# A graph network on one core: messages are added at the rank of their node instead of at an edge that claimed it

## The reference

```python
h = jnp.maximum(_layernorm(x), 0)
x = x + L0(src, dst, h)         # out = (msg + scaled) * dinv; msg: sum over edges, by src, of scaled[dst]
h = jnp.maximum(_layernorm(x), 0)
x = x + L1(h, [src, dst], edge_attr_4, edge_attr_16)
```

```python
r = silu(silu(silu(edge_rbf @ M1) @ M2) @ M3);  tpw = (r @ M4).reshape(-1, 4, C)
msg0 = segment_sum(m0e, rcv, n); msg1 = segment_sum(m1e, rcv, n)   # rcv is dst
A0, A1 = msg0 @ W_lin0, msg1 @ W_lin1
B0, B1 = polynomials of A0 and vv = sum(A1 * A1)
o0, o1 = B0 @ WB0 + h0 @ Wsc0, B1 @ WB1 + h1 @ Wsc1
# then mean and variance of o over all nodes, and a norm with them
```

## Time and profile before

| | us |
|---|---|
| median of 3 runs | 2388.08 (2364.14 to 2389.84) |
| the profiled execution | 2398.8, its span 2396.7 |
| PE, DVE, ACT, POOL busy | 1849.3, 1786.8, 1525.1, 1182.2 |
| DMA moved | 437.47 MB, 183 GB/s |
| granted clock of TensorE, mean | 0.904 of full |

### The profile page before, as it was taken

One profiled execution on the slowest core, in us unless ns is written; L12 is line 12 of the kernel. 1 busy time (PEld: TensorE's weight loads), 2 busy tenths in 40 slices (PEclk: granted clock), 3 DMA queues, 4 the chain that ended last, 5 costly groups with the idle time before them and its releaser, 6 DMA issues.

```text
span 2396.7 us, 54201 instructions
## 1 busy us (share of the span) xinstructions
PE 1849.3 (77%) x14326; PEld 1465.7 (61%) x14326; DVE 1786.8 (75%) x7877; ACT 1525.1 (64%) x3485; POOL 1182.2 (49%) x1159
## 2 busy tenths in 40 slices
PE   6967888888888978999996677776999677777200
PEld 4645666666665655777775566665888677777200
DVE  6764776767676756788784888885998799999663
ACT  4753655556565644777785666655999789999100
POOL 2134555545454432777774777765442121212565
PEclk9987998999899987999997999997999899999655
DMA  5673544445555433777773666655777588888775
GB/s 169 238 182 113 178 173 163 173 166 177 174 175 175 172 131 125 156 163 161 158 152 66 119 120 119 119 102 171 242 245 237 204 288 289 288 289 278 251 228 172
DMA packets 209488, 437.47 MB, mean 183 GB/s; under 512 B 51948, under 2 KB 90377, under 8 KB 209418
## 3 DMA queue, kind: packets, MB, share of 16 engines
q1 hardware_dynamic: 136730, 361.16, 44.0%
q0 software_dynamic: 59584, 74.91, 16.9%
q10 hardware_dynamic: 13104, 0.61, 0.6%
HBM read 220.08 MB, written 219.00 MB: 183 GB/s over the span
## 4 chain that ended last, share of the span: by engine, by line
PE 31%; issue 22%; ACT 18%; POOL 9%; DVE 8%; DMA 6%; another core or an unknown queue 2%; SPq 2%; ACTq 1%; DVEq 0%; POOLq 0%
PE bank L792 16%; ACT hb L1063 6%; PE bank L772 5%; POOL big L502 4%; POOL x_tab L513 3%; PE bank L788 3%; PE bank L751 2%; ACT ht L1212 2%; ACT h L1063 2%; POOL msg_tab L513 2%; PE bank L718 2%; PE bank L729 1%; DVE st L1319 1%; PE bank L736 1%
## 5 line engine op out<-in xcount | busy, mean ns | idle before, releaser
L792 PE MATMUL bank<-w_sb,ht 128*128 128x256 f32 x1568 | 448.4, 429 | 35.7 <-issue 34.5
L792 PEld LDWEIGHTS bank<-w_sb,ht 128*128 128x128 f32 x1568 | 311.3, 209 | 143.0 <-issue 104.4
L1319 DVE BATCH_NORM_STATS2 st<-big 128x6 f32<-128x256 f32 x882 | 314.5, 412 | 93.3 <-DMA big<-x_tab,idx 75.5
L1035 ACT COPY ht<-bank 128x512 f32<-128x512 f32 x196 | 107.9, 588 | 321.9 <-PE bank L772 250.3
L772 PE MATMUL bank<-ident,hb 128*128 128x128 f32 x1568 | 216.4, 281 | 96.7 <-ACT hb L1063 75.0
L1397 DVE SCALAR_TENSOR_TENSOR x1b<-bank,dinv,big 128x64 f32<-128x64 f32 x392 | 109.9, 280 | 223.2 <-PE bank L792 133.5
L502 POOL DMA_INDIRECT big<-x_tab,idx x196 | 192.8, 983 | 141.9 <-ACT h L1063 66.4
L772 PEld LDWEIGHTS bank<-ident,hb 128*128 128x128 f32 x1568 | 181.0, 144 | 131.0 <-issue 96.5
L481 POOL DMA_INDIRECT node_edge<-node_tab,idx x196 | 188.2, 960 | 132.0 <-DVE x1b L1399 74.2
L557 POOL TENSOR_TENSOR big<-big,bias 128x256 f32<-128x256 f32 x98 | 71.6, 730 | 323.5 <-ACT hb L1063 284.2
L1024 ACT ACTIVATE hb<-big,rs 128x256 f32<-128x256 f32 x392 | 207.5, 590 | 18.3 <-DVE rs L1342 16.6
(11 more groups left out here) (241 smaller groups left out, 4514.5 us busy)
## 6 DMA issues: line engine op xcount, KB each, us to landing
big<-in_x_dram SPq DMA_DIRECT2D x97, 512.0 KB
x_tab<-x1b SPq DMA_DIRECT2D x97, 512.0 KB
big<-x_tab SPq DMA_DIRECT2D x97, 512.0 KB
out_dram<-x1b SPq DMA_DIRECT2D x97, 512.0 KB, 2.9
x_odd<-x1b SPq DMA_DIRECT2D x48, 512.0 KB
big<-x_odd SPq DMA_DIRECT2D x48, 512.0 KB
msg_tab<-zeros SPq DMA_DIRECT2D x50, 256.0 KB, 2.2
tpw_tab<-tpb SPq DMA_DIRECT2D x49, 256.0 KB, 2.0
```

Of the source, the lines that this page charges most:

```text
L792: last = mm(y, ht[:, q, (2 * j + k) * P:(2 * j + k + 1) * P], w_sb[:, k, :], start=False, stop=(j == 1 and k == 1))
L1319: last = v.bn_stats(st[:, k, j, :], row)
```

## The change

- `claim_tab`, the claims, the winners, `lead`, `lead_now` and `final_idx` are gone.
- Behind the count, DVE marks the nodes that any edge ends at (`has_dst`, from bank 0). PE counts them by column (four products with one output column each, `in_column`), counts for each node the marked ones on lower partitions of its column (one product with `later`, 392 columns), and adds the marked ones of all columns before (four more products of 392 columns, with the new mask `columns_later`). The sum is the node's rank. DVE turns it into a row number that puts rank r on partition r mod 128 and edge column r // 128, and stores it as a third value in `of_node`.
- `node_tab` rows have three values. POOL gathers the 98 columns of dst rows first, copies the ranks to integers, then for each column scatters dst to `list_tab[rank]`, waiting for the last one to land, and gathers the src row: 98 scatters and 196 gathers, three a group. `list_tab` is cleared with the number of a row of `x1_tab` that holds zeros (N + 256); SP reads it back as column 0 of `idx3`.
- E2 adds messages at the rank. E3 gathers the nodes of the list, each once: the first 78 columns are full, the 79th has 83 nodes, and columns 80 to 98 all read the one row of zeros. F scatters by the list; the numbers beyond the output fall to the bounds check.

```diff
@@ named tables and tiles
-        claim_tab = dram("claim_tab", [G * NG, 1], I32)
-        node_tab = dram("node_tab", [G * NG, 2])
+        list_tab = dram("list_tab", [EDGES, 1], I32)
+        node_tab = dram("node_tab", [G * NG, 3])
+        columns_later = sb("columns_later", [G, J, G * J])
...
@@ POOL, constants before the first mark
+            const(g.memset(columns_later[:], 1.0))
...
+            const(g.affine_select(out=columns_later[:], in_=columns_later[:], compare_op=ALU.is_gt, fill=0.0, base=0,
+                                  pattern=[[-G, J], [1, G * J]], channel_multiplier=-1))
...
@@ POOL, during P1
-                if n % 4 == 0 and n // 4 > 3:
-                    pool.wait_ge(p1["x1"].sem, 2 * (n // 4 - 3))
+                if n % 3 == 0 and n // 3 > 3:
+                    pool.wait_ge(p1["x1"].sem, 2 * (n // 3 - 3))
...
+            run_written_out(T, 0, dst_step)
+            pool.wait_ge(node_in[0].sem, 16 * T)
+            settle(pool)
+            place(g.tensor_copy(rank_i[:], node_edge[:, :, 0, 2]))
+            pool.wait_ge(pre["list_cleared"].sem, 16)
...
+                pace(T + 2 * t)
+                landed(pool, list_out, s, 1)
+                pool.indirect_dma_start(list_tab, rows_of(rank_i[:, t:t + 1]), idx3[:, 1, t:t + 1], None
+                                        ).then_inc(list_out[0].sem, 16)
+                pace(T + 2 * t + 1)
+                of_node_step(1, t)
...
@@ POOL, E3 and F
-                    gather(e3_got, s, 1, x1_tab, e3_free)
+                    gather(e3_got, s, 0, x1_tab, e3_free)
-                    pool.indirect_dma_start(out, rows_of(final_idx[:, t:t + 1]), f_rows[s.slot(0, 4)][:, i, :],
+                    pool.indirect_dma_start(out, rows_of(idx3[:, 0, t:t + 1]), f_rows[s.slot(0, 4)][:, i, :],
...
@@ SP, behind the loads of the weights, and in E1
-            sp.dma_start(claim_tab.rearrange("(p a) d -> p (a d)", p=P),
-                         node_ok[:].bitcast(I32)).then_inc(pre["claim_cleared"].sem, 16)
+            sp.dma_start(list_tab.rearrange("(p a) d -> p (a d)", p=P), no_node[:]).then_inc(pre["list_cleared"].sem, 16)
+            sp.dma_start(x1_tab[N + 2 * P:N + 3 * P, :], zeros[:, 0:D]).then_inc(pre["cleared"].sem, 16)
...
+            all_landed(sp, list_out, T)
+            sp.dma_start(idx3[:, 0, :], list_tab.rearrange("(p t) d -> p (t d)", p=P)).then_inc(pre["list_in"].sem, 16)
@@ PE, between the count and P1
+            pe.wait_ge(pre["has_dst"].sem, 1)
+            for k in range(J):
+                last = mm(bank[6][0:G, k:k + 1], has_dst[:, k * G:(k + 1) * G], ones[:, 0:1], start=True, stop=True)
+            last.then_inc(pre["in_column"].sem, 1)
+            mm(bank[5][:, 0:G * J], later[:, 0, 0:P], has_dst[:], start=True, stop=False)
+            pe.wait_ge(pre["in_column_sb"].sem, 1)
+            for k in range(J):
+                last = mm(bank[5][:, 0:G * J], in_column[:, k:k + 1].to_broadcast([G, P]), columns_later[:, k, :],
+                          start=False, stop=(k == J - 1))
+            last.then_inc(pre["rank"].sem, 1)
@@ PE, E3
-                            last = mm(bank[7][to:to + 1, at], lead_now[:, s.slot(6, 4), i:i + 1],
+                            last = mm(bank[7][to:to + 1, at], ones[:, 0:1],
@@ DVE, degrees
+            v.tensor_scalar(has_dst[:], ends, 0.0, None, ALU.is_gt).then_inc(pre["has_dst"].sem, 1)
...
+            dve.wait_ge(pre["in_column"].sem, 1)
+            v.tensor_copy(in_column[:], bank[6][0:G, 0:J]).then_inc(pre["in_column_sb"].sem, 1)
             dve.wait_ge(pre["root"].sem, 1)
             link(v.reciprocal(dinv, deg[:]))
+            dve.wait_ge(pre["rank"].sem, 1)
+            v.tensor_scalar(of_node[:, :, 2], bank[5][:, 0:G * J], float(T), None, ALU.mult)
+            link(v.tensor_copy(rank_hi[:], bank[5][:, 0:G * J]))
+            link(v.tensor_scalar(rank_hi[:], rank_hi[:], 7, None, ALU.logical_shift_right))
+            link(v.scalar_tensor_tensor(out=of_node[:, :, 2], in0=rank_hi[:], scalar=float(1 - EDGES),
+                                        in1=of_node[:, :, 2], op0=ALU.mult, op1=ALU.add))
             v.tensor_tensor(dinv2[:], dinv, dinv, ALU.mult).then_inc(pre["dinv"].sem, 1)
@@ DVE, start of E1, and E3
-            dve.wait_ge(win_in[0].sem, 16 * T)
-            one(v.tensor_copy(winner[:], winner_i[:]))
-            from_trash(win_delta, winner, 1)
...
+            one(v.tensor_copy(rank[:], node_edge[:, :, 0, 2]))
+            from_trash(rank_delta, rank, 1)
-                    v.tensor_copy(lead_now[:, s.slot(3, 4), :], pair(lead, s, 3)).then_inc(e3["lead_now"].sem, 1)
```

More of the change, by code:

```diff
@@ L189, in build @@
         trash = sb("trash", [P, 2, 2])
[L190 to L193, removed]
+        no_node = sb("no_node", [P, T], I32)
+        rank_i = sb("rank_i", [P, T], I32)
+        rank = sb("rank", [P, T])
+        rank_hi = sb("rank_hi", [P, G * J], I32)
+        has_dst = sb("has_dst", [P, G * J])
+        columns_later = sb("columns_later", [G, J, G * J])
+        in_column = sb("in_column", [G, J])
         valid = sb("valid", [P, T])
@@ L229, in build @@
         deg = sb("deg", [P, G * J])
[L230 removed]
+        of_node = sb("of_node", [P, G * J, 3])
         dinv2 = sb("dinv2", [P, G * J])
@@ L352, in build @@
         EDGES_LOADED = 16 * len(edge_loads)
-        CLEARED = 16 * (S + 2)
-        pre = named("pre", "dve_chain consts edges mlp inputs prepared b3 claim_cleared cleared deg root dinv dinv_out")
+        CLEARED = 16 * (S + 3)
+        pre = named("pre", "dve_chain consts edges mlp inputs prepared b3 list_cleared cleared deg root dinv dinv_out has_dst "
+                           "in_column in_column_sb rank place list_in")
         cnt = named("cnt", "rbf onehot counted turned0 act0 layer1 act1 layer2 act2 layer3 act3 layer4 weights")
@@ L462, in pace @@
             def pace(n):
-                if n % 4 == 0 and n // 4 > 3:
-                    pool.wait_ge(p1["x1"].sem, 2 * (n // 4 - 3))
-            def claim_step(s):
-                t = s.k
-                if t == 0:
-                    pool.wait_ge(pre["prepared"].sem, 1)
-                    pool.wait_ge(pre["claim_cleared"].sem, 16)
-                    pool.wait_ge(p1["x1"].sem, 2)
-                pace(3 * t)
-                landed(pool, claim_out, s, 1)
-                pool.indirect_dma_start(claim_tab, rows_of(idx3[:, 0, t:t + 1]), edge_i[:, t:t + 1],
-                                        None).then_inc(claim_out[0].sem, 16)
-                if t == 0:
-                    pool.wait_ge(pre["dinv_out"].sem, 16)
-                for i in range(2):
-                    pace(3 * t + 1 + i)
-                    pool.indirect_dma_start(node_edge[:, t, i, :], None, node_tab, rows_of(idx3[:, i + 1, t:t + 1])
-                                            ).then_inc(node_in[0].sem, 16)
@@ new lines, in of_node_step, with dst_step @@
+            def of_node_step(i, t):
+                pool.indirect_dma_start(node_edge[:, t, i, :], None, node_tab, rows_of(idx3[:, i + 1, t:t + 1])
+                                        ).then_inc(node_in[0].sem, 16)
+            def dst_step(s):
+                pace(s.k)
+                of_node_step(0, s.k)
+            pool.wait_ge(pre["prepared"].sem, 1)
+            pool.wait_ge(p1["x1"].sem, 2)
+            pool.wait_ge(pre["dinv_out"].sem, 16)
+            run_written_out(T, 0, dst_step)
@@ L496, in gather @@
+            run_written_out(T, 0, list_step)
             def gather(got_sems, s, which, table, free):
@@ L1467, in _ @@
             dve.wait_ge(node_in[0].sem, 16 * 2 * T)
[L1468 to L1477 removed]
+            one = Chain(dve, e2["chain_d"])
+            one(v.tensor_copy(rank[:], node_edge[:, :, 0, 2]))
+            from_trash(rank_delta, rank, 1)
             def e1_step(s):
```

46 lines of the change are left out of this document (11 added, 35 removed).

## The result

The first timing gave 2253.01 us (2247.06 to 2260.07, six runs) beside 2384.05 us for before (six runs): a ratio of 0.9464, 95% interval 0.9432 to 0.9495. The forecast was 2399 us and "the same". It was wrong by 146 us, and the time fell outside its range.

What follows compares the result with a forecast made beforehand. It saw one chain until 141.6 us, then PE busiest in P1 and E3, POOL in E1, E2 and mostly F. Terms 6.7 + 6.7 - 1.2 - 1 = +11.2 us on the median 2388.08 gave 2399 us, range 2370 to 2430.

Steps and rivals of the forecast that it cites:

- P1: In P1, POOL issues 294 small DMAs instead of 392, which nobody there waits for or is slowed by: 0 us.
- Rival A: POOL's small DMAs slow P1 and a quarter fewer give back 33 us of PE's idle time: 2366 us, chance 0.12.
- The counter-argument from DVE's equal durations: DVE's 192-column operation took 0.46 us without POOL DMAs and 463 ns in P1's mean, so contention seemed unlikely.
- Constants: Before P1, two more POOL operations on 1568 columns delay SP's loads and the first store of `tpb`: +6.7 us.
- The rank: Before P1, PE's added products and DVE's operations for the rank delay the first moments: +6.7 us (+4 to +9.4).
- Into E1: Between P1 and E1, a cast and two subtraction halves remain of DVE's eight operations: -1.2 us.
- E1, E2: POOL keeps the same four DMAs a step in both stages, and rank spreads rows as src does: 0 us.
- E3: In E3, DVE loses a copy a step, but PE sets the pace: -1 us (0 to -4).
- F: In F, POOL's issue is unchanged and the last 19 scatters write nothing: 0 us (-8 to +20).
- B: In E3's last 19 columns all reads hit one zero row; at worst 85 us slower, 2484 us, chance 0.07.
- C: F is held by its writes: 2427 us, chance 0.13; sign: DVE waiting for output landings in F's first 39 steps.
- D: The preparation before P1 overlaps more than forecast: +6 us in all, 2394 us, inside the forecast, no separate chance.

Runs made afterwards that it cites:

- a_none: The kernel after with all 294 small GpSimd DMAs held until P1's last group; 2632.92 us in one run, P1 587.9 us.
- b_half: The kernel before with its four small DMAs a group released two by each half group of P1; 2359.47 us, 0.9893 of before.
- a_x16: The kernel after with a fourth small gather, of 16 rows, in each group of P1; 2418.66 us, 1.0028 of before.

## Why the prediction was wrong, and where it was right

- **P1, taken as 0: this step failed.** It rested on two stretches of the earlier trace rows, the one with 12 DMAs and PE busy for 17.0 us, the other with 8 and 12.9. "POOL follows the groups; the poor stretch had fewer DMAs" was true and proved nothing: a starved group is long, so DMAs per microsecond are few in it. What the runs showed in its place: P1 took 625.1 us for 783.9, 159 less. The number that should have been read is DMAs a group, and the order in time: behind the runs of eight DMAs in before PE's first gap comes 5.1 to 5.3 us after their start. The gaps of PE ended by "issue", 43 us in the 460 us from 240 to 700, had a row in the view of waits and none in the prediction.
- **Rival A (0.12) was the mechanism, mis-sized.** It took the price as proportional to the number of DMAs, a quarter of 131 us, 33. The runs show no price up to three a group (48.5 us for eight with none and with three) and all of it above (about 60 with four), so that a quarter fewer gave back most of it (P1 625.1 us, the floor 587.9). It gave more than the 131 us of idle time, because the products themselves got shorter: L792's busy time fell from 448.4 to 398.6 us as the clock stayed high. The counter-argument from DVE's equal durations was weak by itself, since the operation that it looked at reads one tensor from SBUF and one from PSUM, and the rule that it cites is about two SBUF inputs; a_none bears it out. But it doesn't exclude gaps between instructions, which leave durations alone.
- **Constants, +6.7: too high.** The zero product came 3.8 us later (4.6 on chip C), and so did the first store of `tpb` (35.27 for 31.47). The memset took the 1.4 expected; the affine select of 1568 columns took 1.53 us, not 4 times 1.24. Timeline of POOL, SP, ACT and PE in after, beside the earlier trace rows:

```profile
2.66 1.40 POOL L424 MEMSET columns_later<- 98x1568 f32 x1
...
6.03 1.53 POOL L432 TENSOR_SCALAR_AFFINE_SELECT columns_later<-columns_later 98x1568 f32<-98x1568 f32 x1
...
35.27 1.10 SPq L601 DMA_DIRECT2D tpw_tab<-tpb  x1
...
39.81 0.65 ACT L1007 COPY tpb<-bank 128x256 f32<-128x256 f32 x2 [5.65 <-DMA tpw_tab<-tpb]
...
140.31 1.19 PE L751 MATMUL bank<-zeros 128*128 128x256 f32 x2 [0.83 <-ACT tpb L1007]
141.29 1.38 PE L755 MATMUL bank<-ones,has_dst 128*98 128x1 f32 x8
142.53 1.66 PE L757 MATMUL bank<-has_dst,later 128*128 128x392 f32 x2
143.98 4.09 PE L760 MATMUL bank<-columns_later,in_column 98*128 98x392 f32 x8
...
151.14 1.41 DVE L1372 BATCH_NORM_STATS2 st<-big 128x6 f32<-128x256 f32 x4
```

- **The rank, +6.7: right within a microsecond.** First moments came 5.8 us later behind the zero product (5.7 on chip C). The four small products took 1.4 for 1.2, the five of 392 columns 5.5 for 6.5 (142.53 to 148.07), at a granted clock of 0.78 in the stretch.
- **Into E1, E1, E2, E3, F.** On chip C: -0.2 for -1.2; E1 +1.0 and E2 +3.3 for 0 (E2 between +1.0 and +3.3 in the six kernels profiled there, after among them); E3 with what follows +0.2 for -1; F's scatters -0.5 for 0. With 10.4 at the start and 0.7 from there to P1's end that is, but for 0.3 at the very end, the 14.6 us by which the profiled executions differ (2199.5 and 2184.9), 9.8 by the medians.
- **Rivals B and C didn't come.** E3 is as long as before. POOL waits more for the stores of the gathered rows (31.1 us for 15.9 in the 210 us of E3), and nothing comes of it. DVE does wait for landings of the output in F, the sign named for C, but before does so too (on chip C 32.9 and 32.7 us), and F's first twenty pairs of scatters stand 2.9 us apart in both. D was near on the start (+8 for 9.6 measured) and would have given 2394.

So every term but P1 was right to 4 us. That the whole fits so well on chip C, +11.2 for +9.8, is in part luck: the start was forecast 3 us too long and E2 3 us too short. On the other chips one wrong zero outweighed them all.

## What to carry to other kernels

Gaps that end in "issue" on several engines at once are a cost with a cause elsewhere: look at what another engine issued in the microseconds before, and count it per unit of work, not per microsecond. If a kernel runs indirect DMAs of GpSimd under dense work of TensorE, spread them to the units of that work, and time it on more than one chip: here a change is worth 5.5% or nothing by the chip. When such DMAs are held back, find out what then comes last; twice here the gain went into the tail ahead of the next stage.

## What the runs showed of the hardware

- On chips A and B and in the first pair, four indirect DMAs of GpSimd in a group of 6 us starve TensorE, down to one matmul in 0.7 us, and VectorE shows "issue" gaps beside it (29 us in the 460 from 240 to 700 in before, 9 in after). With three, or on chip D with three and one plain DMA, they don't. 16 rows and 128 rows count alike. On chip C nothing of it shows at 320 DMAs in 460 us.
- The price begins just above three a group: 48.5 us for eight groups with 24 DMAs, 48.5 to 53.6 with 25 to 28, about 60 with 32. It costs the granted clock too (1.00 to 0.92 or 0.90 in the mean, 0.50 behind a spell).
- On those chips every run of six and more DMAs with four a group has a gap of PE in or behind it (b_half 22 of 22, a_x16 27 of 27).
- What differs between the chips, what it is that TensorE lacks in a spell, and how much of the price is the number of DMAs and how much the unbroken run, stays open. 3.5 a group was run on chip C alone.
